# A four-layer decoder on one core: expert weights streamed through rings, four chunks in flight, norms' last step on ScalarE, softmax sums inverted once per batch

## The chip, the cores and the metric

One core of a Trainium2 chip runs the whole program. The metric is the device time of one execution in microseconds (us); the engines are TensorE (PE in the profile, PEld for its weight loads), VectorE (DVE), ScalarE (ACT), GpSimd (POOL) and SyncE (SP, which only issues DMAs here).

## The reference

The input x is 8 batches of 256 tokens of width 128, all in float32. It passes through ten sublayers, each followed by a layernorm over the width (a sum with the residual first):

```
ret   retention, 8 heads: (QK' * decay) V, per-head norm, gate, out projection
x0    cross attention over 64 context tokens, 16 heads, masked
moe0  8 experts of 128 -> 512 -> 128, top 2:  relu(x W1[e] + b1) W2[e] + b2, gated and summed
cos   cosine attention block with a 128 -> 128 -> 512 -> 128 relu part
one   attention over key and value matrices of the context
moe1  8 experts of 128 -> 256 -> 128, the same form
spm   sparsemax attention (a threshold instead of a softmax)
x2    cross attention
lora  linear layer with gated low-rank parts
big   attention with 32 heads of 32: softmax(q k' / sqrt 32) v, w_out, layernorm with gamma and beta
x3    cross attention, then a last quantised (ternary) linear layer over everything, "last"
```

All experts are computed for all tokens (the gate is 0 where an expert isn't chosen).

## The kernel before

**Chunks and turns.** The 8 batches are 4 chunks of 2 batches (512 tokens). Each stage of a chunk is written, for each engine, as a generator that yields between its slots (`STAGE_SLOTS`: 11 for `moe0`, 23 for `big`, 504 turns in all for the four chunks). One string, `TURNS`, says turn by turn which chunk goes on by one slot, and `run` walks it for PE, ACT, DVE and POOL alike. So every engine has one fixed order of instructions, and a wait in it holds up all chunks behind it. At most three chunks are in flight: `LIVE = 3` buffers of `XT` (the chunk transposed) and `XB`, and an arena in SBUF in which `places` gives each stage of each chunk its room.

**PSUM.** `Psum.take` hands out the 8 banks in rotation. A product takes the next bank that is not still being filled, and PE waits until the last reader of that bank is done.

**Weights.** All weights lie in SBUF (`WS`), loaded by SP at the start in seven groups: the 12,288 columns of the experts among them.

**End of a stage.** `end_sum_dve` adds the residual and takes the statistics (L447 to L452); POOL takes the power -0.5 (`norm_rstd`, L457); DVE applies mean and scale in four instructions (`norm_apply`, L464); PE transposes (`end_pe`, L490) and ACT copies to `XT` (`end_act`, L495). `end_slots_*` put statistics in the last slot but one and the rest in the last.

**moe.** Slot e of PE runs `hidden_pe(e + 1)` (L1111, four matmuls of 128x512 in moe0, two in moe1) and `sum_pe(e)` (L1127). The relus go to ACT (L1160), of moe0 every fourth to DVE (L1169).

**big.** A turn handles 4 heads (n of 16 in a chunk). PE: `maxima(n+1)` (L1835, into 2 x 2 banks), `scores(n)` (L1853, which waits for `shift_copy`, L1934, then L1858, into 2 x 2 banks), `values(n-1)` (L1870 for E times V, L1874 for the sums of E, spread over 32 rows by `ones32`, in the same bank), `project(n+3)` (L1819 to L1824, 2 banks), `shifts(n+1)` (1 bank). ACT: two exps (L1950) and the copies (L1922 to L1934). DVE: maxima of the scores (L1969), two small ones (L1974, L1976), and `divide(n-1)`: a reciprocal of 128x256 (L1983) and a multiplication (L1987).

Of the kernel before, what the change touches and what calls it, by code (L numbers as in the profile page):

```python
# [31 lines left out]
P = 128  # L32
# [6 lines left out]
LIVE = 3  # L39
OUTS = 12  # L40
# [4 lines left out]
               "big": 23, "x3": 11}  # L45
# [5 lines left out]
    "00000000000000010000000001010001001100000101011101000001010101010101101202022002210212022102201210120102020212"  # L51
    "01021200121201221210212012102110201102100101010201010000101210002020102000000000000000000001001111000201010200"
    "20102001122112212233112333333323133232123231212232323311322313133212313121232222323232311212321323113221232132"
    "32323231232132132323132131311111111111311113311123131333112131331211112131123322323222323222232322323223223233"
    "2323333323233233223232322332323333333333333333333333333333333333"
# [62 lines left out]
W_TOTAL = _at  # L118
# [113 lines left out]
def decoder(nc, x, ctx_t, ctx_d, keep0, keep3, weights, bcols, rows, b2s, out):  # L232
    ctx = ExitStack()
    with ctx:
# [5 lines left out]
        w_loaded = [sem(f"w_loaded{g}") for g in range(len(W_COLS))]  # L240
        small_loaded, consts_made, x_stored = sem("small_loaded"), sem("consts_made"), sem("x_stored")
# [15 lines left out]
        WS = sb("WS", [P, W_TOTAL])  # L257
        W = lambda n: WS[:, W_AT[n][0]:W_AT[n][0] + W_AT[n][1]]
# [8 lines left out]
        ones32 = sb("ones32", [P, 32])  # L267
# [30 lines left out]
        rstd = sb("rstd", [P, 16])  # L298
        ARENA = (nc.sbuf_bytes_remaining - 64) // 4
# [32 lines left out]

        with nc.Block(no_gpsimd_drain=True) as block:
            @block.sync
            def _(sp):
                sp.dma_start(XALL[:, 0:4], x[:, 0:4]).then_inc(x_loaded[0], 16)
                sp.dma_start(WS[:, GROUP_AT[0]:GROUP_AT[1]], weights[:, GROUP_AT[0]:GROUP_AT[1]]).then_inc(w_loaded[0], 16)
# [12 lines left out]
                for g in range(1, len(W_COLS)):  # L350
                    a, b = GROUP_AT[g], GROUP_AT[g + 1]
                    sp.dma_start(WS[:, a:b], weights[:, a:b]).then_inc(w_loaded[g], 16)
# [4 lines left out]
            def _(pool):  # L357
# [6 lines left out]
                pool.memset(ones32[:], 1.0).then_inc(setup_step, 1)  # L364
# [8 lines left out]
                pool.wait_ge(setup_step, 20)  # L373
# [3 lines left out]
                pool.wait_ge(setup_step, 21)  # L377
# [3 lines left out]
                pool.wait_ge(setup_step, 22)  # L381
# [7 lines left out]
                pool.wait_ge(setup_step, 32)  # L389

            @block.scalar
            def _(act):

                act.wait_ge(setup_step, 19)
                for h in range(8):
                    nc.scalar.activation(decay[:, h, :], decay[:, h, :], ACT.Exp,
                                         scale=float(np.log(GAMMA[RET_ORDER[h]]))).then_inc(consts_made, 1)

            @block.vector
            def _(dve):  # L400

                dve.wait_ge(setup_step, 24)
# [12 lines left out]
                for col, value in enumerate((1e9, 1e8)):  # L415
# [10 lines left out]
                                        ALU.add).then_inc(heads_made, 1)  # L426

# [31 lines left out]

        def norm_apply(dve, i, src, dst, name, ready=None):  # L460
# [22 lines left out]
        def end_norm_dve(dve, L, i):  # L483
            norm_apply(dve, i, R[:, i], xc(i), L, L + ".x")
# [47 lines left out]
        def end_slots_act(act, L, i):  # L532
            yield
            end_act(act, L, i)
            yield

        def end_slots_dve(dve, L, i, product=None, base=None):
            end_sum_dve(dve, L, i, product, base)
            yield
            end_norm_dve(dve, L, i)  # L540
            yield

        def end_slots_pool(pool, L, i):
            norm_rstd(pool, i, L)
            yield
            yield
# [22 lines left out]
        def ret_pe(pe, i):  # L569
# [13 lines left out]
            w0 = W_AT["L0_attn_Wv"][0]  # L583
# [174 lines left out]
        class Cross:  # L758
# [287 lines left out]
            def pool(self, pool, i):  # L1046
# [8 lines left out]
                yield from idle(6)  # L1055
                norm_rstd(pool, i, L)
                yield
# [9 lines left out]
        class Moe:  # L1067
            def __init__(self, i, L, prefix, before, group1, group2, J, b2, top2):
                self.L, self.p, self.before, self.g1, self.g2, self.J, self.b2, self.top2 = \
                    L, prefix, before, group1, group2, J, b2, top2  # L1070
# [7 lines left out]
                self.W1 = W(prefix + "_W1").rearrange("p (e j h) -> p e j h", e=8, j=J)  # L1078
                self.W2 = W(prefix + "_W2").rearrange("p (e j d) -> p e j d", e=8, j=J)

            def pe(self, pe, i):
# [9 lines left out]
                pe.wait_ge(w_loaded[self.g1], 16)  # L1091
# [6 lines left out]
                pe.wait_ge(w_loaded[self.g2], 16)  # L1098
# [9 lines left out]
            def hidden_pe(self, pe, i, e):  # L1108
                for j in range(self.J):
                    v = psum.take(pe, f"{self.L}.h{i}.{e}.{j}")  # L1110
                    PE.matmul(v, self.W1[:, e, j], XT[:, slot(i)], start=True, stop=True)\  # L1111
                        .then_inc(psum.filled(f"{self.L}.h{i}.{e}.{j}"), 1)

            def sum_pe(self, pe, i, e):
# [10 lines left out]
                for t in range(4):  # L1125
                    for j in range(self.J):
                        ins = PE.matmul(v[:, tile(t)], self.HT[:, e % 2, j, tile(t)], self.W2[:, e, j],  # L1127
                                        start=j == 0, stop=j == self.J - 1)
                ins.then_inc(psum.filled(f"{L}.y{i}.{e}"), 1)

# [5 lines left out]
            def act_share(self, j):  # L1136

                return j % 4 != 3
# [149 lines left out]
        def cos_pe(pe, i):  # L1288
            cos = cos_at[i]
            pe.wait_ge(w_loaded[3], 16)  # L1290
            w0 = W_AT["L1_attn_Wq"][0]
# [64 lines left out]
        def cos_act(act, i):  # L1356
# [44 lines left out]
            for j in range(0, 4, 2):  # L1401
# [6 lines left out]
        def cos_dve(dve, i):  # L1408
# [41 lines left out]
            for j in (1, 3):  # L1450
                dve.eng.wait_ge(*psum.made(f"cos.h2{i}.{j}"))
                V.tensor_scalar(cos.H2[:, j], psum.view(f"cos.h2{i}.{j}"), bcol("L1_attn_b2", j), 0.0,
                                ALU.add, ALU.max).then_inc(dve.read(f"cos.h2{i}.{j}"), 1)
# [241 lines left out]
        def lora_pe(pe, i):  # L1695
            lora = lora_at[i]
            w0 = W_AT["L2_ffn_gate_w"][0]
# [110 lines left out]
        def big_pe(pe, i):  # L1808
# [53 lines left out]
            def values(n):  # L1862
# [3 lines left out]
                v = psum.take(pe, f"big.o{i}.{n}")  # L1866

# [378 lines left out]
```

## Time and profile before

| | |
|---|---|
| median of 3 runs | 1569.95 us (1566.36 to 1571.66) |
| the profiled execution | 1570.36 us, span of the core 1568.6 us |
| PE busy | 1227.6 us, 78% |
| DVE busy | 1095.4 us, 70% |
| ACT busy | 542.3 us, 35% |
| POOL busy | 150.0 us, 10% |
| TensorE's granted clock, mean | 0.888 of full speed |
| DMA | 16.6 MB, nearly all in the first 45 us |

Busy times are unions per engine; the difference to the span is idle time, which the view of waits puts down to an instruction of another engine. A line such as L464 is that of a helper that many stages use.

### The profile page before, as it was taken

What the parts mean: (1) busy time and instruction counts of PE and PEld (TensorE: products, weight loads), DVE (VectorE), ACT (ScalarE), POOL (GpSimd) and SP (SyncE); (2) the same over time, 40 slices, a digit from 0 to 9 for tenths busy, and PEclk for the clock granted to TensorE, in tenths of its full rate; (3) what the DMA queues carried; (4) which work ended last, traced back from release to release, by engine and by line L of the source; (5) the groups of instructions that cost most, each with busy time, mean ns of one, the idle gap of its engine ahead of it and who ended that gap; (6) DMA issues with size and microseconds to landing.
All of it is one profiled execution on the core that took longest, in us unless ns stands there. A gap on an engine that the chain in (4) does not pass through costs nothing.

```text
span 1568.6 us, 26271 instructions
## 1 busy us (share of the span) xinstructions
PE 1227.6 (78%) x10240; PEld 858.2 (55%) x10240; DVE 1095.4 (70%) x2717; ACT 542.3 (35%) x989; POOL 150.0 (10%) x163
## 2 busy tenths in 40 slices
PE   3589789898989889866888978889786765778851
PEld 2357556666666566644565756566554434556530
DVE  3443566578855777688979976777678788577747
ACT  1132333343332554431323343553343330345410
POOL 3200211101011000202010021000100001100011
PEclk9589889898999999985989988999988887889985
DMA  8000000000000000000000000000000000000000
GB/s 319 37 1 1 1 1 1 1 1 1 1 1 1 1 2 1 1 1 1 1 1 1 1 1 1 2 2 1 1 1 1 1 1 1 1 1 2 2 1 27
DMA packets 5136, 16.61 MB, mean 11 GB/s; under 512 B 2568, under 2 KB 2712, under 8 KB 4376
## 3 DMA queue, kind: packets, MB, share of 16 engines
q1 hardware_dynamic: 5016, 14.94, 2.4%
q8 instruction: 83, 1.36, 0.4%
q14 instruction: 37, 0.30, 0.1%
HBM read 13.89 MB, written 1.05 MB: 10 GB/s over the span
## 4 chain that ended last, share of the span: by engine, by line
PE 57%; DVE 23%; issue 9%; ACT 7%; POOL 2%; DVEq 0%; ACTq 0%; POOLq 0%
PE banks L1127 10%; PE banks L1111 9%; PE banks L1870 4%; PE banks L1858 4%; PE banks L1874 3%; DVE arena L1675 3%; DVE arena L1674 3%; DVE XALL L464 2%; PE banks L866 2%; ACT arena L928 2%; DVE st L447 2%; DVE arena L1983 2%; PE banks L880 2%; PE banks L1853 1%; PE banks L1883 1%
## 5 line engine op out<-in xcount | busy, mean ns | idle before, releaser
L1127 PEld LDWEIGHTS banks<-WS,arena 128*128 128x128 f32 x1536 | 181.9, 193 | 32.2 <-issue 31.2
L1127 PE MATMUL banks<-WS,arena 128*128 128x128 f32 x1536 | 184.1, 277 | 7.4 <-DVE arena L1169 7.4
L1111 PE MATMUL banks<-XT,WS 128*128 128x512 f32 x384 | 181.5, 609 | 0.0
L1160 ACT ACTIVATE arena<-banks,BC 128x512 f32<-128x512 f32 x160 | 108.4, 687 | 174.9 <-PE banks L1111 174.7
L1983 DVE RECIPROCAL arena<-banks 128x256 f32<-128x256 f32 x64 | 112.5, 1757 | 78.6 <-PE banks L1874 78.5
L457 POOL TENSOR_TENSOR rstd<-var,minus_half 128x4 f32<-128x4 f32 x56 | 57.2, 1021 | 1147.6 <-DVE var L452 1147.6
L1969 DVE TENSOR_REDUCE arena<-banks 128x4 f32<-128x1024 f32 x128 | 150.6, 1218 | 23.0 <-PE banks L1835 21.4
L1950 ACT ACTIVATE arena<-banks 128x1024 f32<-128x1024 f32 x128 | 124.8, 1021 | 96.8 <-PE banks L1858 96.8
L524 ACT COPY arena<-banks 128x512 f32<-128x512 f32 x108 | 61.5, 588 | 197.7 <-PE banks L519 53.6
L1200 DVE SCALAR_TENSOR_TENSOR R<-banks,arena,R 128x128 f32<-128x128 f32 x256 | 72.1, 344 | 76.6 <-PE banks L1127 74.8
L1111 PEld LDWEIGHTS banks<-XT,WS 128*128 128x128 f32 x384 | 70.4, 196 | 68.7 <-issue 68.2
L1674 DVE TENSOR_TENSOR arena<-arena 128x512 f32<-128x512 f32 x144 | 100.1, 695 | 4.0
L1675 DVE TENSOR_TENSOR arena<-arena 128x512 f32<-128x512 f32 x144 | 100.5, 698 | 0.0
L490 PE MATMUL banks<-ident,XALL 128*128 128x128 f32 x160 | 36.1, 368 | 78.7 <-DVE XALL L464 76.6
L1870 PE MATMUL banks<-arena 128*32 128x256 f32 x1024 | 75.2, 415 | 24.9 <-DVE arena L1969 24.6
L1858 PE MATMUL banks<-arena 32*128 32x256 f32 x1024 | 89.4, 380 | 0.0
L495 ACT COPY XT<-banks 128x512 f32<-128x512 f32 x44 | 25.8, 587 | 171.6 <-PE banks L490 160.1
L1853 PE MATMUL banks<-arena,ones 32*128 32x512 bf16 x256 | 42.1, 387 | 51.5 <-ACT arena L1934 46.7
L1922 ACT CAST arena<-banks 128x512 bf16<-128x512 f32 x64 | 37.5, 586 | 117.2 <-issue 102.4
L1858 PEld LDWEIGHTS banks<-arena 32*128 32x128 f32 x1024 | 71.4, 189 | 4.6
L1874 PE MATMUL banks<-arena,ones 128*32 128x256 f32 x1024 | 72.7, 403 | 0.0
L490 PEld LDWEIGHTS banks<-ident,XALL 128*128 128x128 f32 x160 | 23.1, 181 | 89.4 <-DVE XALL L464 86.1
(299 smaller groups left out, 2192.3 us busy)
## 6 DMA issues: line engine op xcount, KB each, us to landing
WS<-in_weights SPq DMA_DIRECT2D x3, 2048.0 KB, 16.7
WS<-in_weights SPq DMA_DIRECT2D x1, 2368.0 KB, 27.3
RW<-in_rows SPq DMA_DIRECT2D x1, 1032.0 KB
XALL<-in_x SPq DMA_DIRECT2D x4, 256.0 KB, 18.0
out_dram<-arena SPq DMA_DIRECT2D x4, 256.0 KB, 2.3
WS<-in_weights SPq DMA_DIRECT2D x1, 900.0 KB, 18.4
WS<-in_weights SPq DMA_DIRECT2D x1, 645.0 KB, 21.5
WS<-in_weights SPq DMA_DIRECT2D x1, 580.0 KB, 4.7
```

Of the source, the lines that this page charges most:

```text
L1111: PE.matmul(v, self.W1[:, e, j], XT[:, slot(i)], start=True, stop=True)\
L1127: ins = PE.matmul(v[:, tile(t)], self.HT[:, e % 2, j, tile(t)], self.W2[:, e, j], start=j == 0, stop=j == self.J - 1)
L1160: A.activation(self.HT[:, e % 2, j], psum.view(f"{self.L}.h{i}.{e}.{j}"), ACT.Relu, bias=bcol(self.p + "_b1", e * self.J + j))\
L1200: ins = V.scalar_tensor_tensor(r[:, t], v[:, tile(t)], self.GW[:, t, e:e + 1], r[:, t], ALU.mult, ALU.add)
L1674: V.tensor_tensor(to[:, :, 0:d], lo, hi, ALU.max).then_inc(dve.step(), 1)
L1675: V.tensor_tensor(to[:, :, partner], lo, hi, ALU.min).then_inc(dve.step(), 1)
L1858: ins = PE.matmul(v[:, hh, kt * S:kt * S + S], big.QK[rows_of, n % 3, S + kt * P:S + kt * P + P], big.QK[rows_of, n % 3, 0:S], start=False ...
L1870: PE.matmul(v[32 * h:32 * h + 32, 0:S], big.VV[:, n % 4, kt, 32 * h:32 * h + 32], big.E[:, n % 2, h, kt, :], start=kt == 0, stop=kt == 1)
L1874: ins = PE.matmul(v[32 * h:32 * h + 32, S:2 * S], ones32[:], big.E[:, n % 2, h, kt, :], start=kt == 0, stop=kt == 1)
L1950: A.activation(big.E[:, n % 2, 2 * pair:2 * pair + 2].rearrange("p a b q -> p a (b q)"), psum.view(f"big.e{i}.{n}.{pair}"), ACT.Exp, scale ...
L1969: V.tensor_reduce(big.mx[:, 2 * pair:2 * pair + 2], v, AX.X, ALU.max, negate=True).then_inc(dve.read(f"big.m{i}.{n}.{pair}"), 1)
L1983: V.reciprocal(big.rc, v[:, S:2 * S]).then_inc(dve.step(), 1)
```

## The change

1. The experts' weights leave `WS`. Each of the two moe layers has a ring of `RING = 3` experts (`WE`); SP loads expert n + 3 when `sum_pe` of expert n is done (`sp`), two DMAs for each expert (256 KB each in moe0, 128 KB in moe1), 64 experts in all. SP walks `TURNS` too.
2. `LIVE = 4`, a new string `TURNS` of 508 turns, and a slot more for `big`.
3. The last step of the norm goes to ACT, as x * rstd + shift in four activations (`end_norm_act`); POOL forms -mean (`norm_mean`) and shift = -mean * rstd (`norm_shift`). This holds for the 40 ends of stages that write x; the three other uses of `norm_apply` stay on DVE.
4. All relus of moe0 (32 that were DVE's) and of cos (8) are ACT's.
5. In big, the sums of the heads of 8 values of n go to one bank (`group_column` picks the row of each), held over 8 turns; one reciprocal each 8 turns (`invert`), and 8 matmuls of 32 rows on 32 columns for each pair of n (`spread`) put it back on 32 rows. ACT copies the undivided products out of PSUM (`hold`), DVE multiplies two at once, 128x512 (`divide`).

```diff
-LIVE = 3
+LIVE = 4
+RING = 3
...
+        def load_expert(sp, m, n):
+            for j in range(2):
+                a, w = W_AT[EXPERTS[2 * m + j]]
+                a, w = a + n % 8 * (w // 8), w // 8
+                sp.dma_start(WE[m][:, n % RING, j], weights[:, a:a + w]).then_inc(expert_loaded[m][n % RING], 16)
...
+        def norm_shift(pool, i, name):
+            pool.eng.wait_ge(*pool.own())
+            G.tensor_tensor(shift[:, tiles_of(i)], mean[:, tiles_of(i)], rstd[:, tiles_of(i)], ALU.mult)\
+                .then_inc(pool.flag(name + ".offset"), 1)
+        def norm_mean(pool, i, name):
+            pool.eng.wait_ge(sig(name + ".var"), i + 1)
+            G.tensor_scalar(mean[:, tiles_of(i)], mv[:, tiles_of(i), 0], -1.0, None, ALU.mult).then_inc(pool.step(), 1)
...
-        def end_norm_dve(dve, L, i):
-            norm_apply(dve, i, R[:, i], xc(i), L, L + ".x")
+        def end_norm_act(act, L, i):
+            act.eng.wait_ge(sig(L + ".offset"), i + 1)
+            for t in range(4):
+                k = 4 * i + t
+                ins = A.activation(xc(i)[:, t], R[:, i, t], ACT.Identity, bias=shift[:, k:k + 1], scale=rstd[:, k:k + 1])
...
             def hidden_pe(self, pe, i, e):
+                n = 8 * i + e
+                pe.wait_ge(expert_loaded[self.m][n % RING], 32 * (n // RING + 1))
...
+            def sp(self, sp, i):
+                yield
+                yield
+                for e in range(8):
+                    n = 8 * i + e + RING
+                    if n < 8 * CHUNKS:
+                        sp.wait_ge(*psum.made(f"{self.L}.y{i}.{e}"))
+                        load_expert(sp, self.m, n)
+                    yield
+                yield
...
             def act_share(self, j):
-                return j % 4 != 3
+                return True
...
-                v = psum.take(pe, f"big.o{i}.{n}")
+                if n % 8 == 0:
+                    psum.take(pe, f"big.sum{i}.{n // 8}")
+                v = psum.view(f"big.sum{i}.{n // 8}")
                 for kt in range(2):
                     for h in range(4):
-                        PE.matmul(v[32 * h:32 * h + 32, 0:S], big.VV[:, n % 4, kt, 32 * h:32 * h + 32],
-                                  big.E[:, n % 2, h, kt, :], start=kt == 0, stop=kt == 1)
+                        ins = PE.matmul(v[32 * h:32 * h + 32, 0:S], group_column[:, n % 8].rearrange("p a c -> p (a c)"),
+                                        big.E[:, n % 2, h, kt, :], start=n % 8 == 0 and kt == 0,
+                                        stop=n % 8 == 7 and kt == 1, skip_group_check=True)
...
+            def spread(b, pairs):
+                pe.wait_ge(*psum.copied(f"big.sum{i}.{b}"))
+                for pair in pairs:
+                    v = psum.take(pe, f"big.r{i}.{b}.{pair}")
+                    for g in (2 * pair, 2 * pair + 1):
+                        for h in range(4):
+                            rows_of = row_group(h)
+                            ins = PE.matmul(v[rows_of, g % 2 * S:g % 2 * S + S], spread_group[rows_of, g],
+                                            big.rc[rows_of], start=True, stop=True)
+                    ins.then_inc(psum.filled(f"big.r{i}.{b}.{pair}"), 1)
...
-                if n == 9:
+                if n in (9, 10):
+                    spread(0, (2 * n - 18, 2 * n - 17))
+                if n == 11:
                     output(0)
...
+            spread(1, range(4))
+            yield
             output(1)
...
+            def hold(n):
+                if n == OUTS:
+                    act.eng.wait_ge(*psum.made(f"big.out{i}.0"))
+                act.eng.wait_ge(*psum.made(f"big.o{i}.{n}"))
+                A.copy(big.OT[:, n % OUTS], psum.view(f"big.o{i}.{n}")[:, 0:S]).then_inc(act.read(f"big.o{i}.{n}"), 1)
...
-                V.reciprocal(big.rc, v[:, S:2 * S]).then_inc(dve.step(), 1)
...
+            def invert(b):
+                dve.eng.wait_ge(*psum.made(f"big.sum{i}.{b}"))
+                V.reciprocal(big.rc, psum.view(f"big.sum{i}.{b}")[:, 0:S]).then_inc(dve.read(f"big.sum{i}.{b}"), 1)
+            def divide(b, pairs):
+                for pair in pairs:
+                    k = (8 * b + 2 * pair) % OUTS
+                    held = big.OT[:, k:k + 2].rearrange("p n q -> p (n q)")
+                    V.tensor_tensor(held, psum.view(f"big.r{i}.{b}.{pair}"), held,
+                                    ALU.mult).then_inc(dve.read(f"big.r{i}.{b}.{pair}"), 1)
```

Counted from the two strings: turns at which the next turn is of the same chunk are 181 of 504 before and 111 of 508 after. Turns with 1, 2, 3 and 4 chunks begun and not ended are 49, 132, 323 and 0 before, 27, 66, 143 and 272 after. Between the last two slots of a stage lie turns of other chunks in 38 of 44 stages before (95 turns in sum) and in 42 after (167). Inside `big` of the last chunk, 22 of 22 moves from slot to slot follow directly before, 14 of 23 after.

## Rows read from the trace of the kernel before

**Rows 1.** The page: busy time, share of the span and instructions of the engines.
```profile
PE 1227.6 (78%) x10240; PEld 858.2 (55%) x10240; DVE 1095.4 (70%) x2717; ACT 542.3 (35%) x989; POOL 150.0 (10%) x163
```
**Rows 2.** The chain that ended last, share of the span by engine.
```profile
PE 57%; DVE 23%; issue 9%; ACT 7%; POOL 2%; DVEq 0%; ACTq 0%; POOLq 0%
```
**Rows 3.** Five stretches: length, busy time (count) by engine, TensorE's clock, DMA.
```profile
0.00:100.00 100.00, 52.14 (x365) 34.12 (x366) 39.08 (x108) 20.12 (x35) 24.69 (x48) 0.77 0.36 140
100.00:650.00 550.00, 491.46 (x3748) 348.32 (x3748) 359.74 (x960) 200.70 (x383) 51.88 (x43) 0.95 0.00 1
650.00:1385.00 735.00, 569.74 (x4782) 399.03 (x4777) 571.19 (x1384) 257.27 (x467) 61.66 (x58) 0.87 0.00 1
1385.00:1492.00 107.00, 89.89 (x1141) 60.71 (x1141) 78.35 (x97) 54.62 (x90) 0.00 (x0) 0.98 0.01 2
1492.00:1568.60 76.60, 24.36 (x214) 15.99 (x212) 47.07 (x172) 9.55 (x14) 11.72 (x14) 0.68 0.04 14
```
**Rows 4.** What PE waited for: us in total, times, longest.
```profile
PE banks L490 <- DVE XALL L464: 76.6, 28, 10.2
PE banks L1853 <- ACT arena L1934: 46.7, 58, 1.1
PE banks L1870 <- DVE arena L1969: 24.6, 6, 4.5
```
**Rows 5.** Timeline, the same instruction in two turns of `big` alone, last chunk.
```profile
1398.86 0.39 PE L1853 MATMUL banks<-arena,ones 32*128 32x512 bf16 x2 [0.87 <-ACT arena L1934]
...
1405.04 0.39 PE L1853 MATMUL banks<-arena,ones 32*128 32x512 bf16 x2 [0.87 <-ACT arena L1934]
```
**Rows 6.** Timeline, `values` in two turns of `big` beside `spm`: start, length, idle before.
```profile
1200.69 1.93 PE L1870 MATMUL banks<-arena 128*32 128x256 f32 x16 [4.50 <-DVE arena L1969]
...
1209.00 1.07 PE L1870 MATMUL banks<-arena 128*32 128x256 f32 x16
```
**Rows 7.** DVE's groups by line: busy us, mean ns, idle before.
```profile
L1983 DVE RECIPROCAL arena<-banks 128x256 f32<-128x256 f32 x64 | 112.5, 1757 | 78.6 <-PE banks L1874 78.5
...
L464 DVE TENSOR_SCALAR XALL<-R,mv,rstd 128x128 f32<-128x128 f32 x176 | 50.9, 354 | 9.6 <-POOL rstd L457 8.6
...
L1987 DVE TENSOR_TENSOR arena<-banks,arena 128x256 f32<-128x256 f32 x64 | 27.1, 424 | 2.2
L1169 DVE TENSOR_SCALAR arena<-banks,BC 128x512 f32<-128x512 f32 x32 | 23.8, 744 | 23.2 <-PE banks L1111 23.2
...
L1452 DVE TENSOR_SCALAR arena<-banks,BC 128x512 f32<-128x512 f32 x8 | 5.9, 747 | 10.7 <-PE banks L1343 10.7
```
**Rows 8.** ACT's groups by line.
```profile
L1160 ACT ACTIVATE arena<-banks,BC 128x512 f32<-128x512 f32 x160 | 108.4, 687 | 174.9 <-PE banks L1111 174.7
...
L1927 ACT COPY arena<-banks 128x256 f32<-128x256 f32 x64 | 25.2, 393 | 0.0
...
L1363 ACT ACTIVATE arena<-arena 128x128 f32<-128x128 f32 x32 | 9.9, 310 | 15.8 <-DVE arena L1414 14.2
```
**Rows 9.** POOL's groups by line.
```profile
L457 POOL TENSOR_TENSOR rstd<-var,minus_half 128x4 f32<-128x4 f32 x56 | 57.2, 1021 | 1147.6 <-DVE var L452 1147.6
...
L367 POOL IOTA expert<- 128x8 f32 x1 | 0.1, 146 | 0.3 <-issue 0.3
```
**Rows 10.** PE's groups by line: moe, `big`, the cross attentions.
```profile
L1111 PE MATMUL banks<-XT,WS 128*128 128x512 f32 x384 | 181.5, 609 | 0.0
...
L1874 PE MATMUL banks<-arena,ones 128*32 128x256 f32 x1024 | 72.7, 403 | 0.0
...
L866 PE MATMUL banks<-arena 32*128 32x256 f32 x384 | 43.8, 433 | 0.0
```
**Rows 11.** Timeline, PE's weight loads at a change of tile shape in `big`.
```profile
1402.14 0.30 PEld L1819 LDWEIGHTS banks<-XT,WS 128*128 128x128 f32 x2 [0.41 <-issue]
```
**Rows 12.** DMA issues: KB of each, median us from issue to landing.
```profile
WS<-in_weights SPq DMA_DIRECT2D x3, 2048.0 KB, 16.7
...
out_dram<-arena SPq DMA_DIRECT2D x4, 256.0 KB, 2.3
```

More of the change, by code:

```diff
@@ L117 @@
 GROUP_AT.append(_at)
-W_TOTAL = _at
+EXPERTS = ("L0_ffn_W1", "L0_ffn_W2", "L1_ffn_W1", "L1_ffn_W2")
+KEPT_GROUPS = [g for g, cols in enumerate(W_COLS) if cols[0][0] not in EXPERTS]
+S_AT, _at = {}, 0
+for _g in KEPT_GROUPS:
+    for _n, _w in W_COLS[_g]:
+        S_AT[_n] = (_at, _w)
+        _at += _w
+S_TOTAL = _at
 B_COLS = [("L0_xattn_bq", 1), ("L0_xattn_bk", 1), ("L0_ffn_b1", 32), ("L1_attn_b1", 1), ("L1_attn_b2", 4),
@@ L240, in decoder @@
         w_loaded = [sem(f"w_loaded{g}") for g in range(len(W_COLS))]
+        expert_loaded = [[sem(f"expert_loaded{m}{k}") for k in range(RING)] for m in range(2)]
         small_loaded, consts_made, x_stored = sem("small_loaded"), sem("consts_made"), sem("x_stored")
@@ L298, in decoder @@
         rstd = sb("rstd", [P, 16])
+        shift = sb("shift", [P, 16])
+        mean = sb("mean", [P, 16])
         ARENA = (nc.sbuf_bytes_remaining - 64) // 4
@@ L539, in end_slots_dve @@
             yield
-            end_norm_dve(dve, L, i)
             yield
         def end_slots_pool(pool, L, i):
+            norm_mean(pool, i, L)
             norm_rstd(pool, i, L)
+            norm_shift(pool, i, L)
             yield
@@ L1055, in pool @@
                 yield from idle(6)
+                if not self.last:
+                    norm_mean(pool, i, L)
                 norm_rstd(pool, i, L)
+                if not self.last:
+                    norm_shift(pool, i, L)
                 yield
@@ L1400, in cos_act @@
             yield
-            for j in range(0, 4, 2):
+            for j in range(4):
                 act.eng.wait_ge(*psum.made(f"cos.h2{i}.{j}"))
@@ L1449, in cos_dve @@
             yield
[L1450 to L1453, printed above, removed]
             yield
@@ L1956, in big_act @@
                     shift_copy(n + 1)
+                if n >= 1:
+                    hold(n - 1)
                 yield
+            yield
             yield
@@ L2021, in big_pool @@
             yield from idle(3)
-            yield from idle(GROUPS + 1)
+            yield from idle(GROUPS + 2)
             norm_rstd(pool, i, "bign")
@@ L2027, in decoder @@
         x0 = [Cross(i, "x0", "L0_xattn", "ret", 0, KEEP0, KEEPC0, 1e9) for i in range(CHUNKS)]
-        moe0 = [Moe(i, "moe0", "L0_ffn", "x0", 1, 2, 4, 0, True) for i in range(CHUNKS)]
-        moe1 = [Moe(i, "moe1", "L1_ffn", "one", 4, 4, 2, 1, False) for i in range(CHUNKS)]
+        moe0 = [Moe(i, "moe0", "L0_ffn", "x0", 4, 0, True) for i in range(CHUNKS)]
+        moe1 = [Moe(i, "moe1", "L1_ffn", "one", 2, 1, False) for i in range(CHUNKS)]
         x2 = [Cross(i, "x2", "L2_xattn", "spm", 5, None, None, 0.0) for i in range(CHUNKS)]
@@ L2181, in _ @@
             def _(sp):
+                live = {}
+                for i, stage in ORDER:
+                    if stage in ("moe0", "moe1"):
+                        if (i, stage) not in live:
+                            live[i, stage] = {"moe0": moe0, "moe1": moe1}[stage][i].sp(sp, i)
+                        next(live[i, stage], None)
                 for c in range(CHUNKS):
```

117 lines of the change are left out of this document (70 added, 47 removed).

## The prediction

> **What bounds the kernel now.** I read five views. First the page's busy times [rows 1]: PE is busy for 1227.6 of the span's 1568.6 us, so 341 us are PE's idle time, and DVE comes next with 70%. Then the chain that ended last [rows 2]: 57% PE, 23% DVE, only 7% ACT. PE sets the time where it has work, and what it lacks otherwise is mostly something of DVE's. Third, the busy times by stretch [rows 3], which show that the idle time is not even. The first 100 us (one chunk, loads, the first ends of stages) lose 48, the last 77 (the last x3 and the ternary layer, nothing beside them) lose 52. Between them lie 1392 us with 491.5 + 569.7 + 89.9 = 1151 us of PE, 82.7%. But from 100 to 650 PE is busy for 89.4%, from 650 to 1385 for only 77.5%. The reader is to see DVE in the same rows: 65% in the first of these, 78% in the second. The clock goes with it, 0.95 against 0.87; both are mixes of the levels 1.2 and 2.4 GHz, so PE ran at the low one in about 10% and 26% of the time.
>
> Fourth, what PE waited for [rows 4]. The largest entry is the end of a stage: in 28 of 40 ends PE waits for the last step of the norm, 76.6 us. The second is in `big`, 58 waits of 0.8 us for the copy of the shifts. Its pattern is that of a turn that follows on one of its own chunk [rows 5]: 6.18 us from one instance to the next, 0.87 of them waiting. Fifth, where `big` runs beside `spm` [rows 6]: PE waits 4.50 us before it can take a bank that DVE's maxima still read, and the 16 matmuls behind the wait take 1.93 us where the next 16 take 1.07.
>
> **The change, DVE.** [rows 7] Reciprocals: 56 of 64 go, 56 x 1.757 = 98.4 us. Multiplications: 64 (27.1 us) become 32 of double width; at 0.744 us for a 128x512 from PSUM that is 23.8, so -3.3. Relus: 23.8 of moe0 and 5.9 of cos go. Norms: 160 of the 176 instructions go, 50.9 x 160/176 = 46.3 us. Sum: -178 us, DVE falls from 1095 to some 918 us. Three instructions more in the setup lie beside loads.
>
> **ACT.** [rows 8] 32 + 8 relus x 0.687 = 27.5; 64 copies of `hold` x 0.393 = 25.2; 160 activations x 0.310 = 49.6. Sum +102, from 542 to 645 us, 44% of the new time. Where `big` runs alone, ACT is busy for 54.6 of 107 us [rows 3], 3.2 us of a turn of 6.18; 0.4 more keeps it under PE. In moe0 four matmuls leave PE at 181.5/384 = 0.47 us each [rows 10] and four relus take 0.69 each, so the last relu ends some 1.3 us behind the last matmul (3 x 0.22 + 0.69); `sum_pe` of the expert before and other chunks' turns cover it. With the cover gone it would be 1.3 x 32 = 42 us; before, with three relus on ACT, that tail was shorter by one gap. I take 0.
>
> **The end of a stage.** Before: power 1.02 us on POOL [rows 9], then four DVE instructions, 50.9/44 = 1.16 us [rows 7]. After: POOL's `norm_mean` before the power and `norm_shift` after it, then four of ACT's, 1.24 us. The trace has no such small POOL instruction: from below 0.146 us (the iota of 8 columns), from above the power itself, 1.02. I take 0.3, nearer to the simple one, since no power is taken. So an end grows by 2 x 0.3 + two handovers and 0.08 of ACT, some 0.9 us (0.5 to 2.3). Exposed it costs that; covered it costs nothing. Covered means turns of other chunks between the last two slots: 95 before, 167 after. If all 28 exposed ends stayed so, it would cost 25 us (64 at the most). Instead I expect the exposed ends to halve, and charge only those of the first chunk alone and of the last one: +3 us.
>
> **PE.** `spread` is 256 matmuls of 32 rows, 256 columns. Nearest are the sums in `big`, 72.7/1024 = 0.071 us each where four run side by side, and those of the cross attentions, 43.8/384 = 0.114 [rows 10]: 18 to 29 us, I take 22. The sums themselves stay, 1024 in number. Each of the 12 calls of `spread` also brings one more change of tile shape; where `big` changes shape now, the weight load stands 0.41 us idle [rows 11], so 12 x 0.41 = 5 us. The Trainium skill (TensorEngine Tiling (Array Packing), Key Properties) says that switching the tiling mode drains TensorE; by that rule the 5 us are due in full, and without it the term would be 22 instead of 27. PE's work in the middle becomes 1151 + 27 = 1178 us. The clock gives some back: if the low level falls from 26% to 10% in the 735 us stretch, 118 us change level, and as PE is busy in part of them only, between 0 and 59 us of work go. I take 25: 1153 us.
>
> **The rings.** An expert's load is issued when its y is done and needed two slots of its own chunk later, and between those slots lie 4 turns of other chunks in the median case, 1 in the worst; a turn is 1569/504 = 3.1 us on average, so with the own turn there are some 15 us, and 6 at the least. The one lone transfer of the trace, 256 KB, lands in 2.3 us; a queue full of 2 MB pieces has 16.7 [rows 12]. Two pieces of 256 KB should take 2.5 to 5 us. So I take nothing, with 10 us of cover in the median. SP waits for the y of each expert in PE's own order, so a load is held up by no later product; the last stores lie behind it. A landing over 6 us begins to cost, one over 15 us costs everywhere.
>
> **The sum.** I take the middle to run as the good stretch does now, at 89.4%, since its two conditions come to hold in all of it: DVE at (918 - 39 - 47)/1290 = 64%, about what it is from 100 to 650, and other chunks' turns between those of a chunk (same-chunk successions fall from 181 to 111). 1153/0.894 = 1290 us. The start is 100 + 2. The end is 76.6 + 1 for the norm + 3 for the last batch of `big`: its reciprocal is as long as before, but instead of one multiplication of 0.42 come a first pair of spread (0.6) and four multiplications of 0.74. Sum 102 + 1290 + 81 = 1473 us of span, against 1568.6; with the 1.8 us around the span (1570.36) 1475 us. The profiled execution lies 0.4 us above the median of the three runs, so no correction: **1475 us**.
>
> **The rivals.**
> *Half the relief.* The waits of [rows 4] are latencies more than DVE's load; ACT's queue takes over as what an end waits for (norm and copy in a row, behind other chunks' exps). The middle reaches 86%: 1153/0.86 = 1341, in all 1526 us. For it: most ends are exposed now though DVE idles 30%. Against: the turns between the slots.
> *Better.* The middle reaches 92%: 1153/0.92 = 1253, in all 1438 us; with the full 59 us of clock (1119/0.92 = 1216) 1401. For it: four chunks instead of three in 272 turns, and DVE below 65% in the moe stages.
> *Banks, slower.* In `big` a turn takes 12 banks of 8 in rotation, 8 of them as pairs. The held sum bank leaves 7, in which only three pairs fit: the second pair of scores then falls on the banks of the first maxima of the same turn. So `scores` waits for DVE's L1969 in every turn, and with it all chunks. Price: in a turn alone about nothing, as PE waits 0.87 us for the shifts there anyway, beside `spm` up to the 4.50 us of [rows 6]. It decides from 95/64 = 1.5 us in each of the 64 turns; at 2.25 us it costs 144, 1619 us. The Trainium skill (Perfetto Trace Analysis, Identifying the Most-Contended Engine and Optimization Strategy) says that the same gap repeating on the engine that should be saturated can mean too few buffers in PSUM; that is this rival, and the trace so far shows it in 6 waits only, 24.6 us [rows 4].
> *The relief does nothing.* The middle keeps 82.7%: 1153/0.827 = 1394, in all 1579 us.
> *Rings late.* If a landing takes 19 us, nearer to the 16.7 than to the 2.3 of [rows 12], 4 us on each of 64 loads: 256 more, 1731 us.
>
> **How the numbers follow.** Near the forecast (1450 to 1500) 0.50, half the relief 0.22, better 0.13, banks 0.07, no relief 0.05, rings 0.03. The range of 8 in 10 leaves out part of the better case and all slower ones: 1425 to 1550. About 0.3% (5 us) is what a measurement of this kernel can tell from no change. Faster by more: 0.50 + 0.22 + 0.13 and a little of the others, 0.87; within it 0.03; slower 0.10.
>
> **What would show it.** DVE's busy time at 915 to 925 us, ACT's at 635 to 650; PE's busy time between 1190 and 1255 with a clock of 0.92 or more; the wait for the last norm step below 50 us and named after ACT; the waits of L1853 for the shift copy below 35 us; no wait of the experts' matmuls for a DMA; PE busy for 88 to 91% in the middle. The prediction is wrong if PE's waits for L1969 grow past 60 us, if ACT's copies or exps become a releaser with 100 us, or if the last chunk's x3 and ternary layer are not the last 77 us.

## The result, and the profile after

The kernel with the change takes 1457.55 us in the median of 4 runs (1451.27 to 1461.37), beside 1570.81 for the kernel before, in 4 runs too. The ratio is 0.9275, 95% interval 0.923 to 0.9321: 7.25% faster, where 1475 (6.1%) was forecast. Two executions of the experiments below, one of e5 (3580 us) and one of e9 (4032 us), are left out of their medians. The page, the same lines as [rows 1], and the chain, as [rows 2]:

```profile
PE 1230.4 (84%) x10752; PEld 858.3 (59%) x10752; DVE 918.5 (63%) x2432; ACT 649.7 (45%) x1253; POOL 170.3 (12%) x242
...
PE 70%; DVE 13%; ACT 8%; issue 6%; POOL 1%; DVEq 0%; ACTq 0%; POOLq 0%
```

TensorE is as busy as before (1227.6), in a span that is 110 us shorter. The whole gain is idle time: 341 us before, 228 now. The stretches, with the columns of [rows 3]; the last cut lies in the last `spread` of the last chunk, some 5 us earlier in the program than the cut at 1492 there:

```profile
0.00:100.00 100.00, 52.24 (x428) 35.01 (x428) 44.80 (x108) 21.95 (x40) 27.13 (x52) 0.85 0.27 100
100.00:650.00 550.00, 530.00 (x3528) 383.38 (x3532) 354.66 (x1082) 264.26 (x539) 81.61 (x98) 0.97 0.14 40
650.00:1375.00 725.00, 618.74 (x6548) 419.73 (x6551) 464.93 (x1051) 352.28 (x658) 47.13 (x74) 0.94 0.01 3
1375.00:1458.70 83.70, 29.40 (x260) 20.19 (x249) 54.10 (x194) 11.20 (x18) 14.38 (x18) 0.66 0.04 13
```

The first 100 us and the last 84 are as lost as before (48 and 54 us of idle time, where they had 48 and 52). The middle is TensorE's to 90.1% (1148.7 of 1275 us), the part from 100 to 650 even to 96.4%. What TensorE waits for, as [rows 4]:

```profile
PE banks L545 <- ACT XALL L535: 58.6, 19, 11.5
PE banks L631 <- PEq L360: 22.6, 1, 22.6
...
PE banks L1902 <- ACT arena L2029: 12.4, 11, 1.6
PE banks L1902 <- ACT arena L2015: 12.0, 21, 0.7
PE banks L1920 <- DVE arena L2066: 9.4, 9, 2.7
...
PE banks L1920 <- ACT arena L2022: 5.4, 7, 1.0
...
PE banks L1938 <- DVE arena L2066: 2.7, 2, 1.5
```

The ends of stages (L545, before L490) wait 19 times instead of 28. The shift copy (L2022, before L1934) has gone from 46.7 us to 5.4. The wait for a bank that the maxima read (L1938 and L1920 for L2066) is 12.1 us where L1870 alone had 24.6. New are waits of the next maxima (L1902) for banks that ScalarE still copies out, by `hold` (L2029) and the values' copy (L2015). The changed instructions:

```profile
L2081 DVE RECIPROCAL arena<-banks 128x256 f32<-128x256 f32 x8 | 14.1, 1758 | 15.3 <-PE banks L1938 15.2
L2090 DVE TENSOR_TENSOR arena<-banks,arena 128x512 f32<-128x512 f32 x32 | 21.0, 687 | 28.5 <-PE banks L1957 28.5
```
```profile
L535 ACT ACTIVATE XALL<-R,shift,rstd 128x128 f32<-128x128 f32 x160 | 65.7, 485 | 53.6 <-POOL shift L499 53.6
L2029 ACT COPY arena<-banks 128x256 f32<-128x256 f32 x64 | 26.1, 407 | 5.5 <-PE banks L1946 5.1
```
```profile
L505 POOL TENSOR_SCALAR mean<-mv 128x4 f32<-128x4 f32 x40 | 10.7, 267 | 715.6 <-DVE var L488 715.6
L499 POOL TENSOR_TENSOR shift<-mean,rstd 128x4 f32<-128x4 f32 x40 | 9.1, 228 | 3.1
```
```profile
L1925 PE MATMUL banks<-arena 32*128 32x256 f32 x1024 | 112.7, 396 | 0.0
L1957 PE MATMUL banks<-arena,spread_group 32*32 32x256 f32 x512 | 30.6, 381 | 1.2 <-DVE arena L2081 1.2
L1902 PE MATMUL banks<-arena 32*128 32x256 bf16 x512 | 41.2, 276 | 31.7 <-ACT arena L2029 12.4 <-ACT arena L2015 12.0 <-issue 5.2
```
```profile
WE<-in_weights SPq DMA_DIRECT2D x64, 256.0 KB, 2.9
WE<-in_weights SPq DMA_DIRECT2D x64, 128.0 KB, 2.2
```

### The profile page after: what moved, and what is told of

Its sections match the earlier page's. It is cut to its first block, busy times and chain, and to the rows that moved or that the text cites. A ratio compares the mean times of both kernels' runs of the same rounds, so it can differ in the third digit from the quotient of the medians.

```text
span 1458.7 us, 27476 instructions
## 1 busy us (share of the span) xinstructions
PE 1230.4 (84%) x10752; PEld 858.3 (59%) x10752; DVE 918.5 (63%) x2432; ACT 649.7 (45%) x1253; POOL 170.3 (12%) x242
## 4 chain that ended last, share of the span: by engine, by line
PE 70%; DVE 13%; ACT 8%; issue 6%; POOL 1%; DVEq 0%; ACTq 0%; POOLq 0%
PE banks L1187 12%; PE banks L1171 11%; PE banks L1925 5%; PE banks L1938 4%; PE banks L1946 3%; DVE arena L2066 2%; ACT XALL L535 2%; PE banks L1967 2%; PE banks L923 2%; PE banks L897 2%; PE banks L545 2%; PE banks L1920 2%; PE banks L661 2%; PE banks L1886 1%; PE banks L937 1%
## 5 line engine op out<-in xcount | busy, mean ns | idle before, releaser
L2066 DVE TENSOR_REDUCE arena<-banks 128x4 f32<-128x1024 f32 x128 | 151.1, 1219 | 106.1 <-PE banks L1902 106.0
L1187 PEld LDWEIGHTS banks<-WE,arena 128*128 128x128 f32 x1536 | 180.0, 192 | 24.4 <-issue 23.3
L1231 ACT ACTIVATE arena<-banks,BC 128x512 f32<-128x512 f32 x192 | 130.5, 688 | 120.2 <-PE banks L1171 119.9
L1187 PE MATMUL banks<-WE,arena 128*128 128x128 f32 x1536 | 182.3, 276 | 0.0
L1171 PE MATMUL banks<-XT,WE 128*128 128x512 f32 x384 | 179.0, 602 | 0.0
L1925 PE MATMUL banks<-arena 32*128 32x256 f32 x1024 | 112.7, 396 | 0.0
L1171 PEld LDWEIGHTS banks<-XT,WE 128*128 128x128 f32 x384 | 69.2, 192 | 69.1 <-issue 67.6
L2010 ACT CAST arena<-banks 128x512 bf16<-128x512 f32 x64 | 37.6, 588 | 132.0 <-PE banks L1887 83.2
L1925 PEld LDWEIGHTS banks<-arena 32*128 32x128 f32 x1024 | 88.2, 197 | 7.0
L535 ACT ACTIVATE XALL<-R,shift,rstd 128x128 f32<-128x128 f32 x160 | 65.7, 485 | 53.6 <-POOL shift L499 53.6
L545 PE MATMUL banks<-ident,XALL 128*128 128x128 f32 x160 | 29.7, 316 | 58.8 <-ACT XALL L535 58.6
L1938 PE MATMUL banks<-arena,group_column 128*32 128x256 f32 x1024 | 76.0, 418 | 2.7 <-DVE arena L2066 2.7
L1074 DVE TENSOR_REDUCE arena<-banks 128x16 f32<-128x1024 f32 x48 | 56.5, 1219 | 24.0 <-PE banks L897 23.4
L1920 PE MATMUL banks<-arena,ones 32*128 32x512 bf16 x256 | 49.2, 398 | 23.0 <-DVE arena L2066 9.4
```

Source lines behind the costliest of these rows:

```text
L535: ins = A.activation(xc(i)[:, t], R[:, i, t], ACT.Identity, bias=shift[:, k:k + 1], scale=rstd[:, k:k + 1])
L1171: PE.matmul(v, self.W[:, n % RING, 0, j], XT[:, slot(i)], start=True, stop=True)\
L1231: A.activation(self.HT[:, e % 2, j], psum.view(f"{self.L}.h{i}.{e}.{j}"), ACT.Relu, bias=bcol(self.p + "_b1", e * self.J + j))\
L1920: PE.matmul(v[:, hh].rearrange("p (a q) -> p a q", a=2), ones16[rows_of, :], bc(big.HL[rows_of, n % 2], 1, 2), start=True, stop=True)
L1925: ins = PE.matmul(v[:, hh, kt * S:kt * S + S], big.QK[rows_of, n % 3, S + kt * P:S + kt * P + P], big.QK[rows_of, n % 3, 0:S], start=False ...
L1938: ins = PE.matmul(v[32 * h:32 * h + 32, 0:S], group_column[:, n % 8].rearrange("p a c -> p (a c)"), big.E[:, n % 2, h, kt, :], start=n % 8 ...
```

## The experiments

Twelve kernels, in three rounds (e1 to e4, e5 to e8, e9 to e12), each beside the kernel before on the same chip; ratios are to before, whose medians were 1567.92, 1571.34 and 1571.45 us. Differences between two experiments are taken from their medians, so those of a few us are within the noise. "Old turns" is the string of before with one turn more for the new slot of `big`, three chunks in flight; "new turns" is that of the change, with four.

**e1: the rings alone.**
```diff
 (the kernel before)
+  experts through rings of 3, loads as in the change; an idle slot in big
```


> The kernel before with one thing changed: the experts come through the rings of 3 (and big has its idle slot more); three chunks in flight, the old turns, the old norms, relus and divisions. Theory A (the rings cost nothing): in the kernel after, a load lands in 2.2 to 2.9 us and PE waits for none; here the first chunk's moe0 goes slot on slot, so its loads have one slot of about 4 us, still more than 2.9: 1565 to 1578 us, within 0.5% of before. Rival B (the rings cost time that the rest of the change hides): each of 16 loads of moe0 and moe1 of a chunk that go slot on slot is late by 1 to 3 us: 1590 us or more, and TensorE's waits name a DMA.

Measured: 1573.03 us, ratio 1.003 (1.0015 to 1.0044). The waits are those of before; only the first instruction of TensorE starts at 22.8 us instead of 18.5, since the setup is longer. So the rings cost nothing of their own, theory A; 4.3 of the 5 us are the start.

**e2 and e3: the operations without the order, the order without the operations.**
```diff
 (e2: the kernel after)
-LIVE = 4, new TURNS
+LIVE = 3, old TURNS
 (e3: the kernel after)
-  end_norm_act, act_share = all, spread / invert / hold
+  norm_apply on VectorE, 3 of 4 relus on ScalarE, a reciprocal in each turn
```


> All new operations (norms and relus on ScalarE, one reciprocal each 8 turns with its sum bank, spread, rings), but three chunks in flight and the old turns with one slot more in big. Theory A (operations and order each carry about half): the 25 us of TensorE's waits for the maxima of big beside spm go, the clock there rises, spread adds 31 us of TensorE and each exposed norm 0.9 us: 1520 to 1545 us. Rival C (the order does all, latencies are the idle time): 1560 to 1600 us, since the new operations only add TensorE work and latency. Rival D (VectorE's relief does all): 1480 us or less.

> The new order (four chunks in flight, the new turns, the rings) with all old operations: norms and relus and reciprocals on VectorE, no sum bank, no spread. Theory A: VectorE is at 1095 us of work again, 72% of the time, TensorE has 31 us less; 1500 to 1530 us. Rival C (the order does all): 1445 to 1470 us. Rival D (VectorE's relief does all): 1555 us or more.

Measured: e2 1692.62 us, ratio 1.0786 (1.0756 to 1.0815); e3 1653.35 us, ratio 1.0519 (1.0481 to 1.0557). No theory had a loss for both. Each half alone is a loss of 8% and 5%; together they gain 7%. VectorE's relief is complete in e2 (921.7 us busy, 55%) and nothing comes of it. The waits, e2's first and then e3's:

```profile
PE banks L545 <- ACT XALL L535: 109.5, 38, 11.3
PE banks L1902 <- ACT arena L2029: 42.7, 34, 1.6
```
```profile
PE banks L547 <- DVE XALL L513: 162.1, 38, 14.1
PE banks L1937 <- DVE arena L2038: 38.8, 11, 4.5
```

In both, nearly every end of a stage is waited for (38 of 40). The other experiments take this apart.

**e4: the division of big undone in the kernel after.**
```diff
-  sum bank, invert each 8 turns, spread, hold, divide of 128x512
+  sums beside the product, reciprocal and multiplication in each turn
```


> The kernel after with only the division of big undone: a reciprocal and a multiplication in each turn on VectorE, sums in the second half of the product's bank, no held bank, no spread, no hold copies. Theory A: VectorE gains 102 us, which sit beside TensorE's work mostly, TensorE loses 31 us and the waits for banks read by hold (12 us) and the maxima: 1455 to 1485 us, a little slower than after or the same. Rival E (the held bank and spread cost more than the reciprocals): 1415 to 1445 us, faster than after. Rival D (VectorE's relief does all): 1510 us or more.

Measured: 1507.79 us, ratio 0.9601 (0.9573 to 0.963), between theory A (1485 at most) and D (1510 at least); e2 speaks against D. The batch is worth 50 us here. TensorE works 11 us less than in the kernel after, but waits for VectorE's maxima 41.9 + 17.4 us and for the shift copy 31.7:

```profile
PE banks L1939 <- DVE arena L2040: 41.9, 13, 4.5
PE banks L1922 <- ACT arena L2004: 31.7, 39, 1.1
...
PE banks L1922 <- DVE arena L2040: 17.4, 7, 5.3
```

**e6: only the last step of the norms back on VectorE, in the new turns** (GpSimd's mean and shift go with it).
```diff
-            end_norm_act(act, L, i)
             end_act(act, L, i)
...
             end_sum_dve(dve, L, i, product, base)
             yield
+            norm_apply(dve, i, R[:, i], xc(i), L, L + ".x")
             yield
```


> The kernel after with only the last step of the 40 norms back on VectorE (and GpSimd's mean and shift gone). VectorE has 46 us more and is at 66%, ScalarE 66 us less, and the chain of an end is about 1.2 us shorter. Theory A (VectorE's load costs where it meets spm and big): 1465 to 1490 us. Rival H (the ends are a latency, VectorE has room): 1435 to 1455 us, faster than after. Rival I (the turns are laid out for exactly these operations, and any other queue breaks them, as the two halves of the change alone suggest): 1500 us or more.

Measured: 1608.02 us, ratio 1.0236 (1.0211 to 1.026): rival I. This one move costs 150 us, though VectorE is busy for only 957.8 us, 60%, and the chain of an end is shorter. The wait for it:

```profile
PE banks L545 <- DVE XALL L511: 149.6, 39, 12.2
```

The timeline shows where it comes from. The same end (the 12th in TensorE's order) in e6; start, length, engine, line, and idle before. First GpSimd and VectorE:

```profile
418.37 1.38 POOL L493 TENSOR_TENSOR rstd<-var,minus_half 128x4 f32<-128x4 f32 x1 [22.56 <-DVE var L488]
```
```profile
422.79 0.68 DVE L1736 TENSOR_TENSOR arena<-arena 128x512 f32<-128x512 f32 x1
423.39 0.68 DVE L526 TENSOR_TENSOR R<-banks,XB 128x512 f32<-128x512 f32 x1
...
430.09 0.68 DVE L1736 TENSOR_TENSOR arena<-arena 128x512 f32<-128x512 f32 x1
430.69 0.68 DVE L1259 TENSOR_TENSOR R<-banks,XALL 128x512 f32<-128x512 f32 x1
431.48 1.12 DVE L1265 SCALAR_TENSOR_TENSOR R<-banks,arena,R 128x128 f32<-128x128 f32 x4
432.52 1.10 DVE L511 TENSOR_SCALAR XALL<-R,mv,rstd 128x128 f32<-128x128 f32 x4
...
433.69 1.11 PE L545 MATMUL banks<-ident,XALL 128*128 128x128 f32 x4 [5.45 <-DVE XALL L511]
```

then the kernel after:

```profile
390.41 3.60 PE L1171 MATMUL banks<-XT,WE 128*128 128x512 f32 x8
391.10 0.41 POOL L499 TENSOR_TENSOR shift<-mean,rstd 128x4 f32<-128x4 f32 x1
...
394.05 0.69 ACT L1231 ACTIVATE arena<-banks,BC 128x512 f32<-128x512 f32 x1 [0.17 <-PE banks L1171]
394.63 1.63 ACT L535 ACTIVATE XALL<-R,shift,rstd 128x128 f32<-128x128 f32 x4
...
395.02 3.84 PE L1187 MATMUL banks<-WE,arena 128*128 128x128 f32 x32
...
398.70 0.60 PE L545 MATMUL banks<-ident,XALL 128*128 128x128 f32 x4
```

In e6 the power is ready at 419.75. The norm starts 12.8 us later, since VectorE's queue has other chunks' turns first: adds of `spm`, another chunk's statistics, more adds, and last the sum of an expert (L1265), whose product TensorE finishes only at the end of the turn before this end (here at 428.23). In the kernel after, ScalarE's part of that turn is the relus, fed by its first matmuls (L1171). Its norm then runs beside L1187, and the transposes follow without a wait. Even where no `spm` is ahead, VectorE has L1265 (1.12 us) and then the norm (1.10) to do when TensorE is there already. The wait of 2.24 or 2.25 us that this makes stands at 5 of the first 13 ends of e6, here the next one. TensorE's four transposes take 1.11 us behind the wait of 5.45, 0.66 behind this one, and 0.60 in the kernel after, where they did not wait:

```profile
446.09 0.66 PE L545 MATMUL banks<-ident,XALL 128*128 128x128 f32 x4 [2.24 <-DVE XALL L511]
```

**e9: the same, but VectorE takes the norm in the slot before** (against e6).
```diff
             end_sum_dve(dve, L, i, product, base)
-            yield
             norm_apply(dve, i, R[:, i], xc(i), L, L + ".x")
+            yield
             yield
```


> The kernel of e6 (new turns, last step of the norm on VectorE), but VectorE takes that step right behind its statistics, in the slot before, and stands still for GpSimd's power there. The work is that of e6. Theory L (in e6 the step waits in VectorE's queue behind other chunks' turns, 150 us of TensorE's waits, not for its own work): the waits for VectorE's norm fall below 70 us and the time to 1480 to 1530 us, though VectorE now stands about 1.2 us in each of 40 ends. Rival M (VectorE's load is what costs, or the standing costs as much): 1590 us or more.

Measured: 1479.38 us, ratio 0.9419 (0.939 to 0.9448): theory L, whose range began at 1480; 129 us less than e6 with the same work (VectorE 960.0 us). VectorE now stands 47.2 us for GpSimd, and that costs little:

```profile
PE banks L545 <- DVE XALL L511: 35.8, 11, 10.2
```
```profile
DVE XALL L511 <- POOL rstd L493: 47.2, 42, 1.1
```

**e7: only the 40 relus back on VectorE, in the new turns.**
```diff
             def act_share(self, j):
-                return True
+                return j % 4 != 3
 (and two of the four relus of cos)
```


> The kernel after with only the 40 relus back on VectorE. In moe0 ScalarE falls from 4 to 3 relus a slot. Theory A: VectorE's queue is busy with spm of other chunks when the relu is due, up to 4 us: 1462 to 1480 us. Rival H (ScalarE's four in a row were late for the sums, the split helps): 1440 to 1455 us. Rival I (fitted turns): 1490 us or more.

Measured: 1466.53 us, ratio 0.934 (0.9316 to 0.9364), in the range of theory A. Its interval touches that of the change (0.923 to 0.9321), so the relus are worth some 9 us by the medians, and that is not well apart from nothing.

**e8 and e11: the old turns with all but the batch, and with nothing but the batch.**
```diff
 (e8: e2 without the batch; e11: e1 with the batch)
```


> Old turns, three chunks in flight, norms and relus on ScalarE, but the old division of big (no held bank, no hold, no spread). It splits the 125 us that the new operations cost in the old turns. Theory J (the held bank and hold do the harm: 43 us of waits for hold and slower packing of big's matmuls): 1575 to 1600 us. Rival K (the norm through GpSimd and ScalarE does it, 110 us of waits at the ends): 1640 us or more.

> Old turns, three in flight, only the division of big new (held sum bank, spread, hold); norms and relus on VectorE. With e1 (1573), e8 (1610) and e2 (1693) it makes the table of the old turns full. If the two losses only add: 1573 + 83 = 1650 to 1665 us. If the held bank is harmless while ScalarE has no norms: 1570 to 1600 us.

Measured: e8 1609.96 us, ratio 1.025 (1.0223 to 1.0276); e11 1645.78 us, ratio 1.0489 (1.0454 to 1.0525). In the old turns norms and relus on ScalarE cost 37 us (1573 to 1610) and the batch costs 73 (e11 against e1) or 83 (e2 against e8): the two nearly add (110 of the 120 us of e2). Both theories of e8 had too large a part for themselves; e11 lies 4 us below the range in which the losses add, and far from the other. The table, medians in us:

| | none | batch | norms, relus | all |
|---|---|---|---|---|
| old turns | 1573 (e1) | 1646 (e11) | 1610 (e8) | 1693 (e2) |
| new turns | 1653 (e3) | 1608 with the relus (e6) | 1508 (e4) | 1458 (after) |

**e10: the old turns with all operations, hold ahead of the copies.**
```diff
+                if n >= 1:
+                    hold(n - 1)
                 if n + 3 < GROUPS:
                     copies(n + 3)
                 if n + 1 < GROUPS:
                     shift_copy(n + 1)
-                if n >= 1:
-                    hold(n - 1)
```


> The kernel of e2 (all new operations, old turns) with hold ahead of the copies. Theory J (in the old turns, big goes slot on slot, so the bank that hold reads is the one that the next maxima take: 43 us of waits): those waits go, 1640 to 1660 us. Rival N (the next reader of a bank takes its place, or the packing of big's matmuls carries the loss): 1675 us or more.

Measured: 1673.77 us, ratio 1.0661 (1.0626 to 1.0696), against 1.0786 of e2, between theory J (1660 at most) and rival N (1675 at least). The 42.7 us for hold are gone and 19 of them are gained; most of the rest went to the next readers of banks, the mechanism of N:

```profile
PE banks L1920 <- DVE arena L2066: 21.7, 22, 3.1
...
PE banks L1920 <- ACT arena L2022: 16.9, 35, 1.0
```

(13.5 and 5.2 us in e2. The maxima's waits for a copy of the projections, L2011, are 9.5 us here and none in e2.)

**e5 and e12: the kernel after with hold first, and with VectorE turning the mean's sign.** e5 has the edit of e10. e12 adds:
```diff
+            V.tensor_scalar(mean[:, tiles_of(i)], mv[:, tiles_of(i), 0], -1.0, None, ALU.mult)
...
-            norm_mean(pool, i, L)
```


> The kernel after with one line moved: ScalarE's hold of the last product stands ahead of the copies of the projections in a turn of big, where ScalarE waits for the projections anyway, instead of behind them. TensorE's instructions and banks are the same. In the trace of after, the next maxima take the bank that hold still reads and wait for it, up to 1.6 us. Theory F (that bank sets the turn): the 12.4 us of waits for hold go and turns of big alone fall from 6.6 to about 6.3 us: 1425 to 1447 us. Rival G (the next reader of a bank takes its place, the copy of the values or of the shifts): 1450 to 1460 us, no change.

> The kernel of e5 (after, hold first), and the mean's sign turned by VectorE behind the variance while GpSimd takes the power, so GpSimd has one instruction less on the way of each end. About 0.3 us shorter at the 19 ends that TensorE waits for: 5 us less than e5, 1440 to 1450 us. Rival: VectorE's 40 instructions (7 us) and the fixed order take it back: 1450 to 1458 us.

Measured: e5 1451.13 us, ratio 0.9228 (0.9206 to 0.9249); e12 1448.91 us, ratio 0.9232 (0.9207 to 0.9256). Both medians lie below 1457.55, but the intervals overlap that of the change, and each other: either may be 0.5% better, which is not shown, and e12 can't be told from e5, though its median lies in the range of its first theory. In e5 the wait for hold went and that for L2066 and L2022 rose from 17.5 (9.4 + 2.7 + 5.4) to 24.9 (13.8 + 1.5 + 9.6), which is theory G rather than F.

## Why the prediction was right, and where its reasons weren't

The number came out near, and so did each large term of its sum; the reason given for the largest of them does not hold. That the middle ran at 90% all the same is, by that reasoning, luck.

**Right: the cost of the pieces.** VectorE was forecast at 918 us and has 918.5; ScalarE at 645 and has 649.7. GpSimd's two small instructions were taken at 0.3 us each and take 0.267 and 0.228. The sum's two large terms held too: a middle of 1153 us of TensorE at 89.4% was forecast, 1148.7 at 90.1% is there. The end was given 81 us, 4 more than before; counted from the last matmul of `values` to the end of the span it takes 86.9 where it took 82.7.

**Right: the rings.** 2.9 and 2.2 us from issue to landing, where 2.5 to 5 were forecast; no wait of the experts' matmuls names a DMA; e1 shows them alone.

**Mis-sized, and cancelling.** `spread` was 27 us and is 30.6: I priced 256 instructions by groups that count each float32 matmul twice (the profile has 512 records of it). Counted rightly, the two rows give 0.142 and 0.228 us for an instruction, 36 to 58 us in all, and 0.120 was measured: the double count was offset by rows that were too dear. The 5 us for changes of shape were a misreading of [rows 11]: the 0.41 us are idle time of the weight loads, while TensorE's matmuls run on (L1874 until 1402.22, L1819 from 1402.14), and the matmuls of `spread` have 1.2 us of idle time before them, all of it for VectorE's reciprocal. The rows can't show whether a change of shape slows the matmuls themselves. The same double count is in the 0.47 us for a matmul of moe0: four of them take 3.60 us (L1171 in the timeline under e6), 0.90 each, so a relu of 0.69 ends before the next matmul does and the tail is one relu, not 1.3 us; the term stays nothing.

The activation of the norm was taken at 0.310 us and takes 0.41 (65.7/160), so an end grows by 1.64 - 1.16 + 0.5, about 1 us. TensorE's scores take 112.7 us, where 89.4 was the figure before, and its maxima 41.2 where they had 26.8. That is 38 us that the prediction did not have. For the maxima it comes with the held bank: 29.0 us in e4 and 29.2 in e3 without it, 41.6 in e11 with it. The scores grow with the held bank in the old turns (105.3 us in e11) and in the new turns without it (107.0 in e3, 108.0 in e4). TensorE's total is as forecast because the rest took less. If each moment is counted once, for the line that began first, `big` is busy for 57 us more than before (405.0 to 461.7, `spread` in it) and everything else, the same instructions, for 54 us less (822.5 to 768.6); the transposes at the ends, for one, went from 36.1 to 29.7 us. That goes with a granted clock of 0.927 on average (0.888 before) and 0.94 to 0.97 in the middle, and it is more than the 25 us I took. How much of it is the clock's was not measured.

**The step that failed: "its two conditions come to hold".** The prediction took VectorE's load and the turns between those of a chunk as the two conditions under which the middle runs like the good stretch. The load is not enough: e2 has VectorE at 55% and is 8% slower than before. Nor are the turns between: e3 has them all and is 5% slower. Nor are the two together: e6 has VectorE at 60% and all the turns between, and is 10% slower than the change, while e9 with the same work on VectorE, at 65%, is fast. What counts is what stands ahead of an instruction in its own engine's queue, in a fixed order, at the turn where TensorE needs it. For the ends that is shown by e6 and e9. For big's banks, e10 moves only a place in a queue and gains 19 us, and the waits of e4 and e11 fit. The rival "half the relief" had the right mechanism, a queue as the thing that an end waits for, but put it on ScalarE, where it turned out short: at 10 of the 19 ends that TensorE waits for after, the norm stood behind other work of ScalarE, and they make 21 of the 58.6 us; at the other 9, with 37.6 us, ScalarE itself waited for GpSimd's shift. Its counterpart, that the old turns would take the new operations badly, none of my cases had.

**The ends.** I expected the exposed ends to halve from 28 and charged 3 us; they are 19. Their wait was to fall below 50 us and is 58.6, since they contain the ends of the first and the last chunk alone, up to 11.5 us, which no other chunk can cover. If every end stays exposed, the step by way of ScalarE costs what was bounded, 25 to 64 us: in the old turns its waits grow from 74.9 (e1) to 109.5 (e2). That the order by itself could bring them to 162.1 (e3), with VectorE doing the step, was in no bound.

**The banks.** The rival had a held bank that makes the scores wait for the maxima in every turn. In the kernel after they do so 9 times, for 9.4 us, and its sign is wrong there; in the old turns it comes nearer. There (e11 against e1) TensorE waits 41.2 us for hold and 18.2 for the maxima in front of the scores; these take the place of the waits for the shift copy (46.4 to 4.4) and in front of `values` (24.6 to 0.6), so that idle time grows by only 15 us. The rest of the 72 us is TensorE's busy time, +57: 30.1 for spread, 16 for the scores and 15 for the maxima, whose pairs run less side by side when the second waits for its bank. Counted in the traces, the two pairs of the maxima run apart in 37 of 64 groups of e11 (36 after, none before), and take 0.78 us where together they take 0.42 to 0.47. The pairs of the scores run apart in 14 (19 after, 6 before), and take 2.3 us where together they take 1.3 to 1.5. In the new turns the same held bank comes with a gain of 50, as one reciprocal of 1.76 us in each turn is gone from VectorE's queue ahead of the maxima (e4: 59 us of waits for them, after: 12), and other chunks' turns stand between two of `big` (that these two carry the 50 us is argued from the waits, not tried one by one). In a turn of `big` alone it costs still. After, the last chunk, with two such turns 6.56 us apart where [rows 5] has 6.18:

```profile
1351.24 1.06 PE L1925 MATMUL banks<-arena 32*128 32x256 f32 x14
...
1356.79 0.42 ACT L2029 COPY arena<-banks 128x256 f32<-128x256 f32 x1
...
1357.26 0.28 PE L1902 MATMUL banks<-arena 32*128 32x256 bf16 x2 [1.16 <-ACT arena L2029]
...
1357.80 1.06 PE L1925 MATMUL banks<-arena 32*128 32x256 f32 x14
```

The second maxima wait for the bank that hold reads, as ScalarE does it last in the turn. TensorE's wait for the shift copy, 0.87 us there before, has gone behind it. The Trainium skill (Perfetto Trace Analysis, Identifying the Most-Contended Engine and Optimization Strategy) says that such a repeating gap can mean too few buffers in PSUM. The trace agrees for these turns, and e10 adds that moving the reader helps less than the wait says: 42.7 us of waits went and 19 us were gained.

**What stays open.** Whether a fourth chunk is needed at all was not tried apart from the string that uses it: an order for three chunks, laid out for the new operations, was not built. Nor was the share of the clock in the 150 us of e6 measured; TensorE's waits at the ends explain 91 of them, and its busy time grew by 52 us at a clock of 0.892, 43 of them outside `big`.

## What to carry to other kernels

Where every engine walks one fixed order, an operation and its place in the order are one thing: a part of such a change can't be judged, or predicted, by taking it alone, and a tuned order has to be laid out again before a cheaper operation pays. Before moving an instruction to another engine, look at what that engine's queue holds for the turn just before the result is needed, and on which product of that turn it depends; an engine at 60% whose last item needs TensorE's last product is later than one at 45% that needs its first. If the instruction must stay, take it a turn earlier and let the engine stand: 47 us of standing bought 129.

## What was not expected of the hardware

A ScalarE activation with a scale and a bias of one value for each partition, 128x128 in SBUF, took 482 ns in the median and 0.41 us each in a row, where the activations at L1363, of the same size, had 0.31 [rows 8]. VectorE's tensor_scalar of that size took 0.29 us each in a row (50.9/176), so the step costs ScalarE 1.64 us where VectorE needs 1.1.
